# A language-model tower on one core: the gate and a test on GpSimd, the sum of the values from a column of ones, and another loop order

## The chip, the cores and the metric

The kernel runs on one NeuronCore of a Trainium2 chip. The metric is the device time of one execution in microseconds (us), lower is better. The engines are named as in the profile: PE (TensorE, matmuls; PEld is its weight loads), DVE (VectorE), ACT (ScalarE), POOL (GpSimd) and SP (SyncE, which here only issues DMAs).

## The reference, cut to what matters

```python
h = tok_ref(x, ...)                                  # two Mamba layers, 16 sequences of 128 tokens
h = h + attn_ref(_layernorm(h), w_qkv, w_proj, b_proj)
h = h + ffn_ref(_layernorm(h), w_in, g_in, w_out, g_out)

# one Mamba layer, D 192, D_INNER 384, D_STATE 16
xr, res = split(rmsnorm(x) @ in_proj_w)
xr = silu(causal_conv(xr, 4 taps) + conv_b)
dt, Bm, Cm = split(xr @ x_proj_w)
delta = softplus(dt @ dt_proj_w + dt_proj_b)
h_t = exp(delta * A) * h_{t-1} + delta * Bm * xr     # along the tokens, for each of 16 states
y = einsum(h, Cm) + xr * D
x = x + (y * silu(res)) @ out_proj_w                 # y * silu(res) is the gate below

# attention, 12 heads of 16, on each sequence
attn = relu(1 + qk + qk**2 / 2)                      # = ((1 + qk)**2 + 1) / 2
attn = attn / sum(attn);  out = (attn @ v) @ w_proj + b_proj

# feed-forward, 8-bit rounding of the rows, ternary weights
up, gate = split(quantised(rmsnorm(x, g_in)) @ w_in_q)
y = silu(gate) * up;  out = quantised(rmsnorm(y, g_out)) @ w_out_q
```

All matmuls of the layers and of the attention are float32; those of the feed-forward part are bfloat16 on small integers.

## The kernel before

The instructions of each engine are written out by hand in the order in which they run; semaphores join the engines, and there is no scheduler. The program has two stages.

**The chunk stage** (to about 256 us) does the two Mamba layers. A chunk is four sequences, 512 columns; there are eight: j = 0 to 3 are layer 0, j = 4 to 7 are layer 1. Inner channels are on the partitions in three groups c = 0, 1, 2. A loop `for i in range(...)` on each engine works on several chunks at once, each step with its own offset from i. Its steps for a chunk j:

- PE: `turn_in` (transposes of the scaled rows), `project_in(j, c)` and `project_gate(j, c)` (input projection, 96 + 96 rows), `project_x`, `project_steps`, `spread_b`, `spread_g`, `spread_c` (rows of B, B times C and C on all partitions), `count_below`, `project_out(j, 0/1)`.
- ACT: `first_tap`, `silu_input`, `take_xp`, `magnitude`, `positive_part`, `exponential`, `one_plus`, `logarithm` (these make delta), `decays`, `silu_gate_in`, `take_xt`, `square_sums`.
- DVE: `convolve` (three taps of each group), `error`, `delta`, `input_times_b`, `memoryless_states`, `scan_first`, `times_c`, `skip`, `b_times_c`, `scale`, `add_h`, and before the change also `gate` and `weakest_below`.
- POOL: `rest`, `step_times_input`, `add_first`, two small steps for the root of the mean square.

States 2 to 16 decay so fast that their old part underflows; `weakest_below`, `count_below` and `raise_flag` test that and set a flag, and `states_*` then skips the loop over them. With these inputs the loop is never run. PSUM has eight banks; each step's bank is a constant (`X_BANKS`, `Z_BANKS`, `S_BANKS`, ...), and a step waits until the bank's last user is done.

**The sequence stage** does attention and feed-forward, sequence by sequence (s = 0 to 15), with one prefix for each group g of four: `turn_x`, `project_qk`, `project_v`. For a sequence: `scores`, `square_scores`, `values`, `take_sums`, `turn_sums`, `divide`, `turn_attention`, `take_attention`, `project`, `add_attention`, `input_stats`, `input_gain`, `largest_input`, POOL's `input_root`, `input_most`, `input_step`, then `round_input`, `turn_input`, `take_input`, `project_up`, `silu_gate`, `hidden`, `gain`, `hidden_root`, `hidden_most`, `round_hidden`, `turn_hidden`, `take_hidden`, `project_down`, `add_ffn`, and the DMA of the result. The 1 in the square's expansion makes each score row need the plain sum of the values as well: `sum_tokens` (DVE) sums the rows over the tokens, `sum_values` (PE) multiplies them with the weights, `take_csum` keeps the sum, and `take_sums` (ACT) adds it as a bias while it empties the bank.

`keep_clock(n, b)` issues n matmuls of the identity with itself into bank b whose result nobody reads. They stand in the order after some of the waits, from the end of the chunk stage on.

## Time and profile before

| | |
|---|---|
| median of 3 runs | 413.48 us (413.07 to 415.75) |
| the profiled execution | 413.99 us, span 412.2 us, mean granted TensorE clock 0.967 |
| PE busy | 369.3 us, 90% of the span |
| PEld busy | 201.4 us, 49% |
| DVE busy | 320.7 us, 78% |
| ACT busy | 304.9 us, 74% |
| POOL busy | 200.1 us, 49% |
| DMA | 7.91 MB, nearly all before 50 us |

The span is from the first to the last instruction; 1.8 us of the profiled execution lie around it. A busy share is an average over two stages that have different limits. In a timeline a start and a duration are given; the duration of a DVE instruction reaches about 0.08 us into the next one, so what an instruction costs its engine is the distance of the starts. Float32 matmuls stand as two instructions each in the trace.

### The profile page before, as it was taken

The numbers are of one execution on the slowest core, as the hardware profiler recorded it, in microseconds if no ns is written. First come the engines' busy times: TensorE is split into PE (matmuls) and PEld (weight loads), VectorE is DVE, ScalarE is ACT, GpSimd is POOL, SyncE is SP. The second block draws the span as 40 slices with busy tenths as digits, with TensorE's granted clock in tenths as the row PEclk, the third lists the DMA queues.
The fourth block names the chain that finished last, engine by engine and source line by source line (L and its number), as shares of the span: only waits on it lengthen the run. The fifth ranks groups of instructions, "written<-read, shape, count | busy, mean of one in ns | idle before, by whom it ended". The sixth has DMA issues, their size and how long they took to land. (4 is left out here: it accounts for less than half of the span.)

```text
span 412.2 us, 6636 instructions
## 1 busy us (share of the span) xinstructions
PE 369.3 (90%) x1882; PEld 201.4 (49%) x1882; DVE 320.7 (78%) x687; ACT 304.9 (74%) x574; POOL 200.1 (49%) x300
## 2 busy tenths in 40 slices
PE   0398998999999999999998898999999999999774
PEld 0233333345354453453634537865765665566553
DVE  3069898799999999989999898454678667577752
ACT  2257999899999989899979792347686777478541
POOL 5537345535435345353653445012447564558872
PEclk9999696899999999999999999699899999999999
DMA  6743000000000000000000000000000000000001
GB/s 149 196 149 72 6 0 2 1 1 2 0 1 2 0 1 0 2 1 0 2 2 0 2 1 2 2 2 0 2 2 13 19 11 2 12 21 21 21 17 33
DMA packets 6879, 7.91 MB, mean 19 GB/s; under 512 B 1566, under 2 KB 5623, under 8 KB 6840
## 3 DMA queue, kind: packets, MB, share of 16 engines
q1 hardware_dynamic: 5238, 5.71, 5.0%
q0 software_dynamic: 768, 1.57, 1.8%
q8 instruction: 17, 0.28, 0.3%
q10 hardware_dynamic: 834, 0.17, 0.2%
q14 instruction: 22, 0.18, 0.1%
HBM read 5.87 MB, written 1.57 MB: 18 GB/s over the span
## 5 line engine op out<-in xcount | busy, mean ns | idle before, releaser
L751 PE MATMUL bank<-ring,win 96*128 96x512 f32 x192 | 99.8, 660 | 2.5 <-issue 1.2
L1468 POOL TENSOR_TENSOR du<-dl,pair 128x512 f32<-128x512 f32 x24 | 30.5, 1273 | 72.2 <-DVE dmin L1793 72.2
L751 PEld LDWEIGHTS bank<-ring,win 96*128 96x128 f32 x192 | 37.0, 207 | 57.6 <-issue 50.5
L1786 DVE SCALAR_TENSOR_TENSOR pair<-bank,cw,pair 128x508 f32<-128x508 f32 (+2 forms) x72 | 52.3, 736 | 10.5 <-ACT pair L311 8.6
L1473 POOL TENSOR_TENSOR arena<-arena 128x512 f32<-128x512 f32 x24 | 30.5, 1272 | 29.2 <-DVE arena L1827 29.2
L877 PEld LDWEIGHTS bank<-wout,pair 128*128 128x128 f32 x192 | 32.6, 199 | 10.5 <-issue 9.8
L1462 POOL TENSOR_TENSOR arena<-arena,dl 128x512 f32<-128x512 f32 x24 | 30.5, 1270 | 14.2 <-DVE dl L1778 14.2
L877 PE MATMUL bank<-wout,pair 128*128 128x192 f32 x192 | 37.1, 347 | 0.0
L499 ACT ACTIVATE du<-bank 128x512 f32<-128x512 f32 x48 | 25.1, 597 | 15.0 <-PE bank L983 7.6
L805 PE MATMUL bank<-dbl,wdt 13*128 13x512 f32 x48 | 27.4, 655 | 4.3 <-issue 1.3
L1814 DVE TENSOR_TENSOR_SCAN arena<-arena 128x512 f32<-128x512 f32 x24 | 29.2, 1217 | 0.0
L311 ACT ACTIVATE pair<-bank,cb,cw 128x512 f32<-128x512 f32 x24 | 18.6, 774 | 12.6 <-PE bank L751 12.6
L1528 POOL TENSOR_TENSOR pair<-pair,gout 128x512 f32<-128x512 f32 x16 | 20.5, 1284 | 7.7 <-issue 5.2
L788 PE MATMUL bank<-pair,wx 128*80 128x512 f32 x48 | 22.2, 599 | 2.0 <-ACT pair L345 1.8
L741 PE MATMUL bank<-ident,ring 128*96 128x128 f32 x64 | 9.2, 291 | 16.5 <-DVE ring L1764 16.5
L925 PE MATMUL bank<-ident 128*128 128x128 f32 x88 | 14.8, 295 | 8.9 <-ACT arena L555 3.1
L1793 DVE CUSTOM_DVE_ANT_0 dl<-du,arena 128x512 f32<-128x512 f32 x24 | 20.3, 845 | 1.4 <-issue 0.7
L341 ACT ACT_TABLE_LOAD x16 | 20.5, 1283 | 0.3
L1444 POOL DMA_INDIRECT h<-emb,idx x16 | 17.7, 1108 | 6.1 <-issue 4.3
L510 ACT ACTIVATE arena<-bank,csum 128x128 f32<-128x128 f32 x48 | 14.1, 368 | 7.7 <-PE bank L995 7.5
L925 PEld LDWEIGHTS bank<-ident 128*128 128x128 f32 x88 | 11.4, 190 | 14.7 <-ACT arena L555 4.5
L1778 DVE SCALAR_TENSOR_TENSOR dl<-du,dl 128x512 f32<-128x512 f32 x24 | 16.6, 692 | 2.0 <-ACT du L336 1.9
(183 smaller groups left out, 872.7 us busy)
## 6 DMA issues: line engine op xcount, KB each, us to landing
out<-h SPq DMA_DIRECT2D x16, 96.0 KB, 1.6
win<-in_w SPq DMA_DIRECT2D x2, 576.0 KB
arena<-ffn_in_t SPq DMA_DIRECT2D x1, 768.0 KB
wout<-out_w SPq DMA_DIRECT2D x2, 288.0 KB
arena<-ffn_out_t SPq DMA_DIRECT2D x1, 384.0 KB
wa<-w_qkv SPq DMA_DIRECT2D x1, 288.0 KB
wb<-w_qkv SPq DMA_DIRECT2D x2, 144.0 KB
h<-emb,idx POOLq DMA_INDIRECT x16, 6.5
```

What stands on the lines that cost most here:

```text
L341: nc.scalar.activation(du[:, j % NG, c, :], du[:, j % NG, c, :], ACT.Ln).then_inc(ln_done, 1)
L499: nc.scalar.activation(sq[s % 2][:, r, :], bank[:, SC_BANKS[r], :], ACT.Square, scale=HD ** -0.5, bias=1.0).then_inc(sq_ready, 1)
L751: last = nc.tensor.matmul(bank[:, b, :], win[:, j // NG, k, m * P:(m + 1) * P], xtr[:, j % 2, k, :], start=(k == 0), stop=(k == KH - 1))
L788: last = nc.tensor.matmul(bank[0:XM, XP_BANK, :], wx[:, j // NG, c, :], xc[:, j % NG, c, :], start=(c == 0), stop=(c == CI - 1))
L805: nc.tensor.matmul(bank[:, S_BANKS[c], :], wdt[DT_AT:DT_AT + R + 1, j // NG, c * P:(c + 1) * P], dbl[DT_AT:DT_AT + R + 1, j % 2, :], start ...
L877: last = nc.tensor.matmul(bank[:, T_BANK + b, i * D:(i + 1) * D], xc[:, j % NG, c, t0:t0 + LEN], wout[:, j // NG, c, :], start=(c == 0), s ...
L925: nc.tensor.matmul(bank[:, b, 0:P], ident[:, :], ident[:, :], start=True, stop=True)
L1462: nc.gpsimd.tensor_tensor(relu_s[:, c, :], relu_s[:, c, :], dl[:, j % NG, c, :], ALU.subtract).then_inc(rest_done, 1)
L1468: nc.gpsimd.tensor_tensor(du[:, g, c, :], dl[:, g, c, :], xc[:, g, c, :], ALU.mult).then_inc(du_ready, 1)
L1473: nc.gpsimd.tensor_tensor(yv[:, c, :], yv[:, c, :], bx[:, c, :], ALU.add).then_inc(yv_done, 1)
L1786: nc.vector.scalar_tensor_tensor(acc, seqs(bank[:, X_BANKS[c], :])[:, :, 0:LEN - tap], cw[:, j // NG, c, TAPS - 1 - tap:TAPS - tap], acc, ...
L1814: nc.vector.tensor_tensor_scan(bx[:, c, :], da[:, c, :], bx[:, c, :], 0.0, ALU.mult, ALU.add).then_inc(scan_done, 1)
```

## The change

Seven things are changed at once.

1. `gate` (a 128x512 multiplication for each chunk and group, 24 in all) and `weakest_below` (24 small ones) are moved from DVE to POOL.
2. The loop bodies of the chunk stage are in another order on every engine, with other PSUM banks and other waits that follow from them.
3. The sum of the values comes from `values` itself: the buffer of squared scores has a 129th column of ones, the matmuls have 129 columns, and `take_sums`, now on DVE, adds the last column to the others. `sum_tokens`, `sum_values`, `take_csum` and `spread_values` are gone.
4. In the sequence stage the 192 rows of a contraction are split 128 + 64 (`project_up` had 96 + 96). The two 64-row parts lie in different halves of the partitions and are issued one after the other. `take_x` copies twice instead of three times. The input projection of the chunk stage remains 96 + 96.
5. The `w_in` of the feed-forward part is laid out as 128 x 1536 instead of 96 x 2048 while it is made ternary.
6. `silu_gate` waits for both halves of `project_up`.
7. `keep_clock` is gone, and the order of the sequence stage is another one on every engine.

```diff
-X_BANKS = (3, 7, 4)
-Z_BANKS = (5, 7, 2)
-S_BANKS = (5, 6, 5)
+X_BANKS = (6, 2, 5)
+Z_BANKS = (3, 6, 3)
+S_BANKS = (5, 3, 7)
...
-                nc.scalar.activation(sq[s % 2][:, r, :], bank[:, SC_BANKS[r], :], ACT.Square, scale=HD ** -0.5,
-                                     bias=1.0).then_inc(sq_ready, 1)
-
-            def take_sums(s):
...
-                act.wait_ge(csum_out, s // SG + 1)
...
-                    nc.scalar.activation(nm[:, s % 2, c, :], bank[:, PV_BANK, c * P:(c + 1) * P], ACT.Identity,
-                                         bias=csum[:, s // SG % 2, c, s % SG:s % SG + 1]).then_inc(nm_out, 1)
+                    nc.scalar.activation(sq[s % 2][:, r, :, 0:P], bank[:, SC_BANKS[r], :].rearrange("p (j n) -> p j n", j=JH),
+                                         ACT.Square, scale=HD ** -0.5, bias=1.0).then_inc(sq_ready, 1)
...
             def project_in(j, c):
                 if c == 0:
-                    if j >= 2:
-                        pe.wait_ge(t_ready, 3 * (j - 1))
+                    if j >= 1:
+                        pe.wait_ge(dbl_ready, j)
+                        pe.wait_ge(bc_ready, j)
...
-            def keep_clock(n, b):
-                for _ in range(n):
-                    nc.tensor.matmul(bank[:, b, 0:P], ident[:, :], ident[:, :], start=True, stop=True)
...
-            def sum_values(g):
...
-                        last = nc.tensor.matmul(bank[j * HS:(j + 1) * HS, PV_BANK, c * P:(c + 1) * P],
-                                                va[b][:, i, c * JH + j, :], sq[s % 2][:, c, j * P:(j + 1) * P],
+                        last = nc.tensor.matmul(bank[j * HS:(j + 1) * HS, PV_BANK, c * (P + 1):(c + 1) * (P + 1)],
+                                                va[b][:, i, c * JH + j, :], sq[s % 2][:, c, j, :],
                                                 start=True, stop=True)
...
             def project_up(s):
                 pe.wait_ge(qxt_ready, s + 1)
-                for half in (1, 0):
-                    for k in range(KH):
-                        last = nc.tensor.matmul(bank[:, U_BANKS[half], :], qxt[:, s % 2, k, :],
-                                                wq1[:, k, half * F:(half + 1) * F], start=(k == 0), stop=(k == KH - 1))
-                    last.then_inc(up_ready, 1)
+                for k, half in enumerate((1, 0)):
+                    nc.tensor.matmul(bank[:, U_BANKS[half], :], qxt[:, s % 2, k, :], wq1[:, k, :], start=True, stop=False)
+                for k, half in enumerate((1, 0)):
+                    r = slice(64 * (1 - k), 64 * (2 - k))
+                    nc.tensor.matmul(bank[:, U_BANKS[half], :], qxt[r, s % 2, 1 - k, :], wq1[r, 2, :],
+                                     start=False, stop=True).then_inc(up_ready, 1)
...
+            def weakest_below(j):
+                if j >= 2:
+                    pool.wait_ge(count_ready, j - 1)
+                for c in range(CI):
+                    pool.wait_ge(delta_ready, 3 * j + c + 1)
+                    nc.gpsimd.tensor_scalar(below[:, j % 2, c:c + 1], dmin[:, j % 2, c:c + 1],
+                                            weakest[:, j // NG, c:c + 1], UNDERFLOW, ALU.mult,
+                                            ALU.is_le).then_inc(below_ready, 1)
+
+            def gate(j, c):
+                pool.wait_ge(scan_dve, (j + 1) * DECAYING * DVE_U)
+                pool.wait_ge(yv_done, 3 * j + c + 1)
+                pool.wait_ge(sz_ready, 3 * j + c + 1)
+                nc.gpsimd.tensor_tensor(xc[:, j % NG, c, :], sz[:, j % NG, c, :], yv[:, c, :],
+                                        ALU.mult).then_inc(gated, 1)
...
+            def ones_scores():
...
+                for b in range(2):
+                    nc.gpsimd.memset(sq[b][:, :, :, P:P + 1], 1.0).then_inc(ones_sq, 1)
...
+            def take_sums(s):
+                if s == 0:
+                    dve.wait_ge(wx_ready, 3)
+                if s >= 2:
+                    dve.wait_ge(nm_turned, s - 1)
+                dve.wait_ge(pv_ready, CH * s + CH)
+                for c in range(CH):
+                    at = c * (P + 1)
+                    nc.vector.tensor_scalar(nm[:, s % 2, c, :], bank[:, PV_BANK, at:at + P],
+                                            bank[:, PV_BANK, at + P:at + P + 1], None, ALU.add).then_inc(nm_out, 1)
```

**POOL in the loop of the chunk stage, before.** L1468 is `step_times_input`, L1462 `rest`, L1473 `add_first`, L1452 and L1457 the root of the mean square.

```order
L1468 TENSOR_TENSOR du<-dl,pair 128x512 x2
L1452 TENSOR_SCALAR ms<-ms 128x4
L1457 TENSOR_TENSOR rstd<-ms,neg_half 128x4
L1462 TENSOR_TENSOR arena<-arena,dl 128x512
L1468 TENSOR_TENSOR du<-dl,pair 128x512
L1473 TENSOR_TENSOR arena<-arena 128x512 x3
```

The same stretch after the change: L1347 is `gate`, L1339 `weakest_below`, L1332 `step_times_input`, L1326 `rest`, L1353 `add_first`.

```order
L1347 TENSOR_TENSOR pair<-pair,arena 128x512 x2
L1332 TENSOR_TENSOR du<-dl,pair 128x512
L1316 TENSOR_SCALAR ms<-ms 128x4
L1332 TENSOR_TENSOR du<-dl,pair 128x512
L1326 TENSOR_TENSOR arena<-arena,dl 128x512
L1321 TENSOR_TENSOR rstd<-ms,neg_half 128x4
L1332 TENSOR_TENSOR du<-dl,pair 128x512
L1347 TENSOR_TENSOR pair<-pair,arena 128x512
L1339 TENSOR_SCALAR below<-dmin,weakest 128x1 x3
L1353 TENSOR_TENSOR arena<-arena 128x512 x2
L1326 TENSOR_TENSOR arena<-arena,dl 128x512
L1353 TENSOR_TENSOR arena<-arena 128x512
```

Twelve full-size instructions a chunk stand there instead of nine, and the gates of groups 0 and 1 come before the next chunk's `step_times_input`, that of group 2 after it.

**PE where the chunk stage ends, before.** L829 is `spread_c(7)`, L941 and L946 `project_qk(0, t)`, L877 x12 `project_out(6, 0)` and `(6, 1)`, L955 and L960 `project_v(0)`, L925 `keep_clock`, L858 `count_below(7)`, L983 `scores(0)`.

```order
L941 MATMUL bank<-dl,wa 96x512 x2
L946 MATMUL bank<-dl,wb 96x512 x2
L829 MATMUL bank<-dbl,picked 128x512
L877 MATMUL bank<-wout,pair 128x192 x12
L955 MATMUL bank<-wa,dl 128x192 x2
L960 MATMUL bank<-wb,dl 128x192 x2
L955 MATMUL bank<-wa,dl 128x192 x2
L960 MATMUL bank<-wb,dl 128x192 x2
L925 MATMUL bank<-ident 128x128 x4
L858 MATMUL bank<-below,ones 128x1 x3
L983 MATMUL bank<-pair 128x256 x6
```

After the change, from `project_gate(7, 0)` and `(7, 1)` on: L674 `project_gate`, L754 `spread_c(7)`, L784 `count_below(7)`, L805 `project_out(6, 0)`, L852 `turn_x(0)`, L805 `project_out(6, 1)`, L862 and L865 `project_qk(0, 0)`.

```order
L674 MATMUL bank<-ring,win 128x512 x4
L754 MATMUL bank<-dbl,picked 128x512
L674 MATMUL bank<-ring,win 128x512 x2
L784 MATMUL bank<-below,ones 128x1 x3
L805 MATMUL bank<-wout,pair 128x192 x6
L852 MATMUL bank<-ident,ring 128x128 x8
L805 MATMUL bank<-wout,pair 128x192 x6
L862 MATMUL bank<-dl,wa 96x512 x2
L865 MATMUL bank<-dl,wb 96x512 x2
```

Before, both parts of `project_qk(0)` and all of `project_v(0)` stand ahead of `count_below(7)`. Now everything of the sequence stage stands behind it, and all three gate projections of chunk 7 are still to be done in its last round.

**PE at the very end, before.** L1046 is `project_down`, L1039 `turn_hidden`.

```order
L1046 MATMUL bank<-wq,arena 128x192 x4
L925 MATMUL bank<-ident 128x128 x4
L1039 MATMUL bank<-ident,pair 128x128 x4
L925 MATMUL bank<-ident 128x128 x2
L1046 MATMUL bank<-wq,arena 128x192 x4
L925 MATMUL bank<-ident 128x128 x3
L1039 MATMUL bank<-ident,pair 128x128 x4
L925 MATMUL bank<-ident 128x128 x2
L1046 MATMUL bank<-wq,arena 128x192 x4
```

And after: L951 `turn_hidden`, L958 `project_down`.

```order
L951 MATMUL bank<-ident,pair 128x128 x4
L958 MATMUL bank<-wq,arena 128x192 x8
L951 MATMUL bank<-ident,pair 128x128 x4
L958 MATMUL bank<-wq,arena 128x192 x4
```

The identity matmuls between a wait and the work behind it are gone (44 in the program), and two `project_down` now stand between the last two `turn_hidden`.

## Rows read from the trace of the kernel before

**Rows 1.** The page's part 2: granted TensorE clock in 40 slices of the span.

```profile
PEclk9999696899999999999999999699899999999999
```

**Rows 2.** Windows: us, busy us of each engine (count), granted clock, DMA share, GB/s.

```profile
57.10:220.00 162.90, 157.08 (x462) 72.01 (x461) 154.07 (x272) 150.13 (x253) 75.74 (x67) 0.97 0.00 1
...
118.97:145.64 26.67, 25.90 (x81) 12.26 (x80) 25.82 (x45) 25.56 (x44) 12.53 (x11) 1.00 0.00 1
...
259.90:267.30 7.40, 7.40 (x52) 5.90 (x55) 2.44 (x8) 1.57 (x3) 0.00 (x0) 0.55 0.00 0
...
262.00:380.00 118.00, 114.37 (x1017) 75.12 (x1015) 75.97 (x230) 78.91 (x183) 56.78 (x135) 0.97 0.03 9
380.00:412.20 32.20, 21.67 (x147) 15.40 (x145) 17.42 (x47) 13.44 (x29) 20.69 (x46) 1.00 0.07 23
```

**Rows 3.** Timeline of PE in a chunk: start, us, instructions of two group projections.

```profile
151.91 3.68 PE L751 MATMUL bank<-ring,win 96*128 96x512 f32 x8
```

**Rows 4.** Timeline of DVE in the same stage, start and us.

```profile
128.12 1.32 DVE L1793 CUSTOM_DVE_ANT_0 dl<-du,arena 128x512 f32<-128x512 f32 x1
...
130.88 0.68 DVE L1875 TENSOR_TENSOR pair<-pair,arena 128x512 f32<-128x512 f32 x1
131.48 0.69 DVE L1778 SCALAR_TENSOR_TENSOR dl<-du,dl 128x512 f32<-128x512 f32 x1
132.08 0.69 DVE L1793 CUSTOM_DVE_ANT_0 dl<-du,arena 128x512 f32<-128x512 f32 x1
```

**Rows 5.** Timeline of POOL beside it.

```profile
127.63 1.27 POOL L1462 TENSOR_TENSOR arena<-arena,dl 128x512 f32<-128x512 f32 x1 [1.46 <-DVE dl L1778]
```

**Rows 6.** Groups by line and shape: busy us, mean ns, idle before.

```profile
L1814 DVE TENSOR_TENSOR_SCAN arena<-arena 128x512 f32<-128x512 f32 x24 | 29.2, 1217 | 0.0
...
L1827 DVE SCALAR_TENSOR_TENSOR arena<-pair,dskip,arena 128x512 f32<-128x512 f32 x24 | 17.7, 738 | 0.0
...
L341 ACT ACT_TABLE_LOAD x16 | 20.5, 1283 | 0.3
...
L510 ACT ACTIVATE arena<-bank,csum 128x128 f32<-128x128 f32 x48 | 14.1, 368 | 7.7 <-PE bank L995 7.5
...
L1755 DVE TENSOR_SCALAR wq<-arena 96x2048 bf16<-96x2048 f32 x1 | 1.4, 1371 | 0.0
```

**Rows 7.** Timeline of PE at the start.

```profile
37.48 1.99 PE L751 MATMUL bank<-ring,win 96*128 96x512 f32 x4
...
41.48 6.97 PE L751 MATMUL bank<-ring,win 96*128 96x512 f32 x8
...
57.10 2.78 PE L788 MATMUL bank<-pair,wx 128*80 128x512 f32 x6
```

**Rows 8.** Timeline of PE where the chunk stage ends.

```profile
219.98 2.77 PE L788 MATMUL bank<-pair,wx 128*80 128x512 f32 x6
...
246.64 4.17 PE L877 MATMUL bank<-wout,pair 128*128 128x192 f32 x24
...
254.96 0.83 PE L858 MATMUL bank<-below,ones 128*128 128x1 f32 x6 [0.51 <-DVE below L1799]
...
268.33 0.52 PE L1003 MATMUL bank<-ident,arena 128*128 128x128 f32 x3
```

**Rows 9.** Timeline of DVE there: the last three gates.

```profile
257.68 1.89 DVE L1875 TENSOR_TENSOR pair<-pair,arena 128x512 f32<-128x512 f32 x3 [1.13 <-POOL arena L1473]
```

**Rows 10.** Timeline of PE in the sequence stage.

```profile
310.98 1.10 PE L946 MATMUL bank<-dl,wb 64*96 64x512 f32 x4
...
312.62 1.85 PE L971 MATMUL bank<-xsum,wvp 128*128 128x4 f32 x12
314.40 1.04 PE L1032 MATMUL bank<-wq,arena 96*128 96x512 bf16 x4
```

**Rows 11.** The chain that ended last, in order of time, near its end.

```profile
390.30 0.71 PE bank L925 x4
...
408.44 0.71 PE bank L925 x4
```

More of the change, by code:

```diff
@@ L1077, in _ @@
             project_qk(0, 1)
[L1078 to L1080 removed]
+            project_out(7, 0)
+            pe.wait_ge(sz_ready, 24)
+            pe.wait_ge(abs_done, 22)
+            pe.wait_ge(relu_done, 22)
+            pe.wait_ge(p_done, 24)
+            scores(0)
             pe.wait_ge(q_out, 4)
@@ L1154, in _ @@
             turn_attention(3)
+            pe.wait_ge(qxt_ready, 1)
+            turn_input(1)
+            pe.wait_ge(nm_out, 15)
+            values(5)
+            pe.wait_ge(att_out, 4)
+            turn_sums(4)
             pe.wait_ge(v_out, 4)
@@ L1956, in _ @@
-                if i - 4 in CHUNKS:
-                    add_h(i - 4, 0)
-                if i - 2 in CHUNKS:
-                    error(i - 2, 0)
+                if i - 2 in CHUNKS:
+                    delta(i - 2, 2)
+                    skip(i - 2, 1)
+                    scan_first(i - 2, 0)
+                if i - 1 in CHUNKS:
+                    b_times_c(i - 1)
+                if i - 2 in CHUNKS:
+                    times_c(i - 2, 0)
+                    scan_first(i - 2, 1)
+                    memoryless_states(i - 2, 2)
+                    times_c(i - 2, 1)
@@ L2109, in add_ffn @@
                                                ALU.mult, ALU.add).then_inc(h_out, 1)
+            convolve(6, 2, 1)
+            convolve(6, 2, 2)
+            input_times_b(5, 0)
+            convolve(6, 2, 3)
+            memoryless_states(5, 0)
+            input_times_b(5, 1)
+            memoryless_states(5, 1)
+            skip(5, 0)
+            scale(7)
+            delta(5, 2)
+            skip(5, 1)
+            scan_first(5, 0)
+            b_times_c(6)
+            times_c(5, 0)
+            scan_first(5, 1)
@@ L2129, in _ @@
-            gate(5, 1)
-            normalise(1)
+            memoryless_states(6, 1)
+            skip(6, 0)
+            delta(6, 2)
+            skip(6, 1)
             scan_first(6, 0)
-            gate(5, 2)
-            skip(6, 0)
-            normalise(2)
+            b_times_c(7)
+            times_c(6, 0)
             scan_first(6, 1)
-            delta(6, 2)
-            times_c(6, 0)
-            memoryless_states(6, 1)
+            memoryless_states(6, 2)
             times_c(6, 1)
+            error(7, 0)
@@ L2308, in _ @@
             round_input(7)
-            sum_tokens(3)
+            take_sums(10)
+            round_input(8)
             add_attention(9)
```

1398 lines of the change are left out of this document (624 added, 774 removed).

## The prediction

> **What bounds the kernel now.** I read the page's busy shares and its clock line first, then the windows by stage, then the timelines where the diff works. The clock line shows full speed but for a few dips [rows 1], so an answer per stage is possible, and there are three.
>
> In the chunk stage one undisturbed chunk takes 26.67 us, and PE is busy for 25.90 of them, DVE for 25.82, ACT for 25.56, POOL for 12.53 only [rows 2]. Three engines are full; relieving one of them leaves two. From `project_x(1)` at 57.10 to `project_x(7)` at 219.98 are 162.9 us, of which PE is busy 157.1 [rows 2, 7, 8]. In the sequence stage (262 to 380) PE has 114.4 of 118 us and the others 79 at most: PE alone bounds it. From 380 on PE has 21.7 of 32.2, nobody is full, and the end is a chain of short steps [rows 2], with `keep_clock` in it [rows 11].
>
> The sum below is made against the profiled execution, 413.99 us, which is 0.5 above the median of the runs.
>
> **Start.** The ternary preparation is four DVE passes over 2048 columns; one takes 1.37 [rows 6], so three quarters of the columns save about 4 x 1.37 x 1/4 = 1.4 us of DVE. But `project_in(1, 0)` now waits for `b_times_c(0)`, and that stands on DVE behind the preparation, near 41.0 by my walk, where it began at 37.48 before [rows 7]: PE stands idle some 3.5 us. The last eight input matmuls of chunk 1 took 6.97 us there at half clock, and 3.68 is what eight take at full clock [rows 3, 7]; with a pause ahead of them the half clock may come again. At full clock `project_x(1)` is reached at 56, at half clock near 62; I take 58.4: **+1.3 us**, with -1 and +5 as ends.
>
> **Chunk loop.** PE's work is the same, 157.1 us for the six chunks, a floor at -5.8. ACT loses two of its five table loads a chunk, 1.28 each [rows 6], so it comes to 23.0. DVE loses three gates, 0.60 from start to start each [rows 4], and the three small tests, 0.4: 2.2 together. What POOL gets is 3 x 1.27 (as its other full-size instructions, rows 5) + 0.6 = 4.4: 12.53 + 4.4 = 16.9 us.
>
> What speaks against this move is in the timelines. A `delta` usually starts 0.60 after its neighbour and is shown with 0.69, but one that started at 128.12, while POOL's `rest` ran from 127.63 to 128.90, is shown with 1.32 and ends 0.54 after POOL's [rows 4, 5]. I found ten such meetings in the stage, about one a chunk, each costing DVE 0.25 to 0.64, and no DVE instruction with two inputs from SBUF that ran through a POOL instruction at its usual speed. So each pair of engines' instructions of that kind must fit in one period: POOL 16.9, and DVE three times error 0.60, delta 0.60, scan 1.13 and skip 0.65 [rows 4, 6] = 8.9, and the scaling of a chunk's rows, under 1: 26.7 us at most. That is just over PE's 25.9. Not all has to be packed to the full, since a DVE instruction that reads PSUM may run beside POOL: DVE without its present stall and gates is 25.82 - 0.6 - 2.2 = 23.0; in the new order I count about four meetings of half a POOL instruction (0.64) = 2.5, so 25.5, still under PE. If three in five of the 12 instructions meet, it is 23.0 + 7.5 x 0.64 = 27.8. I take a period of 26.2, between PE's 25.9 and the port's 26.7; with 1.7 of PE's busy time over 6 x 25.9 it is 158.9 against 162.9: **-4.0 us**, ends -5.8 and +5.6.
>
> The Trainium skill, "SBUF — State Buffer", section "SBUF: two separate sides", describes this: DVE and GpSimd share one port pair under an exclusive lock, a DVE instruction with two SBUF inputs takes it only against a GpSimd instruction that reads SBUF, and the loser blocks for the whole instruction. The trace agrees (end 0.54 after POOL's end). By it alone and with no slack the period would be the port sum.
>
> **Transition**, from `project_x(7)` to the first `turn_sums`, 48.35 us before [rows 8]. `count_below(7)` ran at +35.0 and now comes at about +34.4, since the deltas of chunk 7 set it either way and PE is idle around it. Behind it stand now: `project_out(6, 0)` and `(6, 1)` at 2.1 each (two take 4.17, rows 8), `turn_x` 1.0, `project_qk` twice at 1.84 + 1.03 (a full part and a packed pair, rows 3, 10), 10.9 in all and 11.2 with a gap: `project_out(7, 0)` at +45.6. The gates are no longer DVE's three in 1.89 [rows 9], which ended at +39.6, but POOL's at 1.27 each, behind `add_first`, `ones_columns`, the root and `ones_scores`: they end near +43.1, late but hidden. Then `project_out(7, 0)` 2.1, `scores(0)` 1.1, `project_v(0)` 2.9, `project_out(7, 1)` 2.1, `values(0)` and part of `scores(1)` 1.6: +55.4. The half-clock stretch 259.9 to 267.3 (clock 0.55, rows 2) cost 7.4 x 0.45 = 3.3 and may come or not; I leave 1.0 for it. That is 56.4, or +8.0; one us comes back later, because `project_out(7, 1)` is then done: **+7.0 us**, ends +3 (no pause, full clock) and +10 (the half clock again).
>
> **Sequence stage.** PE-bound, so PE's work counts. `sum_values` goes: 1.85 each for the three groups of the stage [rows 10], -5.6. `project_up` has two full matmuls and a packed pair in place of four that take 1.04 [rows 10]; a packed pair of 64 rows takes 1.03 where four unpacked ones take 1.84 [rows 3, 10], so 0.1 to 0.2 a sequence, -2.7 for 16. That makes -8.3; the column of ones adds 12 columns' worth a sequence, next to nothing. ACT loses 48 `take_sums` of 0.37 [rows 6], DVE gets them for about as much less `sum_tokens`: 76 + 8 of 118 us, not the bound. I take **-7.5**; ends -3, if waits replace half of it, and -10, if the dip of the clock near 295 [rows 1] goes too.
>
> **Tail.** Ten `keep_clock` pieces stand on the chain from 390.3 to 409, 0.71 for most, 7.9 us in all [rows 11]. Without them PE has little to do there, and may fall to half clock: the rest of its work on the chain is 6 us, so up to +6, of which I take 4.5. `silu_gate` waits for the second half of `project_up` as well, +0.4 in all, and 1.0 because POOL's steps are next: -7.9 + 4.5 + 0.4 + 1.0 = **-2.0 us**, ends -7 and +1.
>
> **Sum:** 1.3 - 4.0 + 7.0 - 7.5 - 2.0 = -5.2, so 408.8 for the profiled execution and **408.3 us** for the median.
>
> **The rivals.** *The port binds the chunk loop.* For it: three engines at 96% and a POOL that collides whenever it is busy; against it: DVE's PSUM readers fit beside POOL. At a period of 27.8 the loop is 9.6 above my value: 417.9 us, slower than before; from 27.1 on (5.2 / 6 above 26.2) it decides the sign.
>
> *The half clock without `keep_clock`.* A stretch of 7 us at half clock costs 3.3 to 3.7 [rows 2, 3 and 7]. Two more of them than I took, at the start, the transition or in the tail, give 415.5 us. For it: the order before has identity matmuls just behind such waits; against it: the dips stood there in spite of them [rows 1].
>
> *Everything packs.* PE works through at full clock, 25.9 a chunk (-1.8 more), a transition at +4 (-3), the dip gone (-2), a tail at -5 (-3): 398.5 us. For it: the new order waits for fewer banks, and ACT and DVE both have 2.5 us of slack a chunk.
>
> *The sequence stage isn't bound by PE alone.* If DVE's share or the banks of `project_up` set the rate, the stage gives 2 instead of 7.5: 413.8 us, no change.
>
> **How the numbers follow.** Forecast 0.35, everything packs 0.25, the port 0.15, the half clock 0.12, the sequence stage 0.13. My forecast's own range is 404 to 412. About 1%, 409.3 to 417.6, is what a measurement of this kernel can tell from no change. Faster: all of packs and seven tenths of the forecast, 0.50; slower: a bit over half the port's and a part of the half clock's cases, which go above 417.6 only with the forecast's own errors, and something for what I haven't seen, 0.21; the rest 0.29. The range reaches from 398 to 418, which leaves out the upper half of the port's cases and the lower third of those in which everything packs.
>
> **What the profile after would show.** `project_x(1)` at 58.4 with an idle gap ahead of `project_in(1, 0)`; `project_x(7)` 158.9 later, one chunk at 26.2, POOL at 16.9 of them; DVE's delta, scan and skip with means above today's 1.22 and 0.74 where POOL runs beside them; the first `turn_sums` 56 after `project_x(7)`; a sequence at half a us less; a clock of 0.5 to 0.7 in the last 20 us. The prediction is wrong if the chunk period is not between 25.9 and 26.7, if PE still fills the transition, or if the tail keeps its clock.

## The result: 9% slower, with long stretches of PE at half clock

The changed kernel takes 450.18 us (449.41 to 451.36, 3 runs) against 413.48 before: a ratio of 1.0875, with an interval of 1.0803 to 1.0946. I had forecast 408.3, in a range that ended at 418. The profiled execution has a span of 447.6 us and a mean granted clock of 0.864 (412.2 and 0.967 before), and 379.0 us of PE busy time where 369.3 stood, although PE has less work.

The clock line of the page, to be laid beside [rows 1]:

```profile
PEclk9998589699955955999889667799999999999965
```

The windows by stage: us, busy us of PE, PEld, DVE, ACT, POOL (count of instructions), granted clock, DMA share, GB/s. The first goes from `project_x(0)` to `project_x(1)`, the next four are single chunks (2, 3, 4 and 5 of the eight), then comes the transition, then the stage of the sequences up to the last `turn_sums`, and the tail.

```profile
32.28:65.48 33.20, 29.16 (x53) 10.58 (x53) 21.33 (x36) 19.95 (x37) 14.40 (x13) 0.69 0.11 22
...
92.94:117.94 25.00, 24.25 (x81) 12.09 (x80) 22.92 (x37) 22.21 (x41) 21.37 (x17) 1.00 0.00 1
117.94:152.69 34.75, 34.17 (x81) 17.99 (x81) 25.55 (x40) 22.34 (x41) 21.27 (x17) 0.71 0.00 0
152.69:187.16 34.47, 34.11 (x81) 17.98 (x80) 25.06 (x39) 22.32 (x41) 21.27 (x17) 0.70 0.00 1
187.16:213.39 26.23, 24.56 (x81) 12.01 (x80) 25.22 (x39) 22.21 (x41) 21.28 (x17) 1.00 0.00 1
...
242.66:304.52 61.86, 48.80 (x202) 31.03 (x203) 41.46 (x82) 25.01 (x40) 36.01 (x32) 0.81 0.00 1
...
304.52:411.68 107.16, 100.20 (x920) 59.91 (x920) 79.82 (x250) 63.83 (x133) 54.67 (x131) 1.00 0.03 9
411.68:447.60 35.92, 20.02 (x97) 10.12 (x97) 18.40 (x50) 13.81 (x28) 20.52 (x47) 0.73 0.07 22
```

At full clock a chunk is shorter than before, 25.00 and 26.23 us against 26.67 [rows 2], and PE is busy for 24.25 and 24.56 us of it, not for 25.90. The largest part of that comes from the new order: it puts `project_steps(j, 2)` (13 rows) right ahead of `spread_g` (16 rows), and the two start within 0.01 us of each other. Before, the first two lines here, they stood 10 us apart, with 1.05 us of PE for each.

```profile
121.55 1.12 PE L805 MATMUL bank<-dbl,wdt 13*128 13x512 f32 x2
131.82 1.12 PE L823 MATMUL bank<-bc,not_first 16*128 16x512 f32 x2
...
102.93 0.69 PE L732 MATMUL bank<-dbl,wdt 13*128 13x512 f32 x1
102.94 0.69 PE L746 MATMUL bank<-bc,not_first 16*128 16x512 f32 x1
```

In chunk 3 the same 81 matmul instructions fill 34.17 us, at a clock of 0.71. Against before the difference is made up so (starts of the same work in both traces; the whole is 447.6 - 412.2 = 35.4):

| part | before | after | difference | forecast |
|---|---|---|---|---|
| to `project_x(1)` | 57.1 | 65.5 | +8.4 | +1.3 |
| `project_x(1)` to `project_x(7)` | 162.9 | 177.2 | +14.3 | -4.0 |
| to the first `turn_sums` | 48.35 | 61.9 | +13.5 | +7.0 |
| to the last `turn_sums` | 113.4 | 107.2 | -6.2 | -7.5 |
| to the end | 30.5 | 35.9 | +5.4 | -2.0 |

What stands ahead of a fall of the clock is plain in PE's timeline, here at the start of chunk 3's round: transposes, two `project_steps` of 13 rows, 0.58 us of waiting for `b_times_c`, and then `project_in`, which takes 3.45 us where 1.98 is usual.

```profile
120.54 1.04 PE L664 MATMUL bank<-ident,ring 128*96 128x128 f32 x8
121.51 1.98 PE L732 MATMUL bank<-dbl,wdt 13*128 13x512 f32 x4
124.06 3.45 PE L674 MATMUL bank<-ring,win 96*128 96x512 f32 x4 [0.58 <-DVE bc L1672]
```

Why was `b_times_c` late? On DVE it stands behind the first scan. In the chunk before, the scan took 1.23 us; here it takes 2.29, and `b_times_c` comes 5.3 us after `project_x` instead of 4.1:

```profile
95.80 1.23 DVE L1709 TENSOR_TENSOR_SCAN arena<-arena 128x512 f32<-128x512 f32 x1 [1.07 <-ACT arena L355]
97.06 0.68 DVE L1672 TENSOR_TENSOR bc<-dbl,bank 16x512 f32<-16x512 f32 x1
...
120.96 2.29 DVE L1709 TENSOR_TENSOR_SCAN arena<-arena 128x512 f32<-128x512 f32 x1
123.28 0.68 DVE L1672 TENSOR_TENSOR bc<-dbl,bank 16x512 f32<-16x512 f32 x1
```

On POOL `step_times_input` and the gate of group 2 run at that time:

```profile
120.45 1.72 POOL L1332 TENSOR_TENSOR du<-dl,pair 128x512 f32<-128x512 f32 x1 [2.54 <-DVE dmin L1695]
122.13 2.19 POOL L1347 TENSOR_TENSOR pair<-pair,arena 128x512 f32<-128x512 f32 x1
```

The scan is shown until 123.25, but by these rows the two engines take turns: the first POOL instruction ends 1.2 us after the scan's start, which is about what the scan is longer than its usual 1.22, and the gate is shown 0.9 longer than the 1.27 of POOL's full-size instructions before. That PE must wait for `b_times_c` at all comes from the new banks: bank 6 holds the result of `project_x` and then the first input projection of the next chunk (before: banks 4 and 3).

By group (busy us, mean ns, idle before), both sides pay now. POOL's instructions were 1270 long and the scan 1217 [rows 5, 6]:

```profile
L1332 POOL TENSOR_TENSOR du<-dl,pair 128x512 f32<-128x512 f32 x24 | 37.1, 1546 | 61.3 <-DVE dmin L1695 61.3
...
L1709 DVE TENSOR_TENSOR_SCAN arena<-arena 128x512 f32<-128x512 f32 x24 | 38.1, 1589 | 3.9 <-ACT arena L355 3.0
```

### The profile page after: what moved, and what is told of

Its sections match the earlier page's. It is cut to its first block and busy times, and to the rows that moved or that the text cites. A ratio compares the mean times of both kernels' runs of the same rounds, so it can differ in the third digit from the quotient of the medians.

```text
span 447.6 us, 6336 instructions
## 1 busy us (share of the span) xinstructions
PE 379.0 (85%) x1746; PEld 201.4 (45%) x1746; DVE 319.8 (71%) x672; ACT 266.9 (60%) x504; POOL 267.9 (60%) x350
## 5 line engine op out<-in xcount | busy, mean ns | idle before, releaser
L674 PE MATMUL bank<-ring,win 96*128 96x512 f32 x192 | 111.3, 725 | 9.5 <-issue 4.0
L1686 DVE SCALAR_TENSOR_TENSOR pair<-bank,cw,pair 128x508 f32<-128x508 f32 (+2 forms) x72 | 52.3, 738 | 31.1 <-ACT pair L299 25.8
L1332 POOL TENSOR_TENSOR du<-dl,pair 128x512 f32<-128x512 f32 x24 | 37.1, 1546 | 61.3 <-DVE dmin L1695 61.3
L674 PEld LDWEIGHTS bank<-ring,win 96*128 96x128 f32 x192 | 41.0, 227 | 72.3 <-issue 62.3
L805 PE MATMUL bank<-wout,pair 128*128 128x192 f32 x192 | 50.0, 429 | 0.0
L805 PEld LDWEIGHTS bank<-wout,pair 128*128 128x128 f32 x192 | 44.6, 259 | 7.8 <-POOL pair L1347 4.5
L1353 POOL TENSOR_TENSOR arena<-arena 128x512 f32<-128x512 f32 x24 | 36.4, 1530 | 9.2 <-DVE arena L1722 8.2
L1709 DVE TENSOR_TENSOR_SCAN arena<-arena 128x512 f32<-128x512 f32 x24 | 38.1, 1589 | 3.9 <-ACT arena L355 3.0
L1326 POOL TENSOR_TENSOR arena<-arena,dl 128x512 f32<-128x512 f32 x24 | 37.1, 1549 | 4.2 <-DVE dl L1678 4.2
L1347 POOL TENSOR_TENSOR pair<-pair,arena 128x512 f32<-128x512 f32 x24 | 36.6, 1537 | 4.9 <-DVEq L1735 4.9
L307 ACT ACTIVATE dl<-bank 128x512 f32<-128x512 f32 x24 | 14.1, 588 | 34.3 <-PE bank L732 34.3
L732 PE MATMUL bank<-dbl,wdt 13*128 13x512 f32 x48 | 28.6, 704 | 1.9 <-DVE arena L1703 1.2
L1775 DVE TENSOR_TENSOR h<-h,bank 128x384 f32<-128x384 f32 x16 | 8.8, 549 | 17.3 <-PE bank L805 16.3
L1394 POOL TENSOR_SCALAR ms<-mv 128x1 f32<-128x1 f32 x16 | 3.6, 227 | 28.8 <-DVE mv L1928 27.8
L509 ACT ACTIVATE pair<-bank,deq 128x512 f32<-128x512 f32 x16 | 11.0, 690 | 14.6 <-PE bank L945 7.2
```

The costliest lines, as they stand in the source:

```text
L674: last = nc.tensor.matmul(bank[:, b, :], win[:, j // NG, k, m * P:(m + 1) * P], xtr[:, j % 2, k, :], start=(k == 0), stop=(k == KH - 1))
L732: nc.tensor.matmul(bank[:, S_BANKS[c], :], wdt[DT_AT:DT_AT + R + 1, j // NG, c * P:(c + 1) * P], dbl[DT_AT:DT_AT + R + 1, j % 2, :], start ...
L805: last = nc.tensor.matmul(bank[:, T_BANK + b, i * D:(i + 1) * D], xc[:, j % NG, c, t0:t0 + LEN], wout[:, j // NG, c, :], start=(c == 0), s ...
L1326: nc.gpsimd.tensor_tensor(relu_s[:, c, :], relu_s[:, c, :], dl[:, j % NG, c, :], ALU.subtract).then_inc(rest_done, 1)
L1332: nc.gpsimd.tensor_tensor(du[:, g, c, :], dl[:, g, c, :], xc[:, g, c, :], ALU.mult).then_inc(du_ready, 1)
L1347: nc.gpsimd.tensor_tensor(xc[:, j % NG, c, :], sz[:, j % NG, c, :], yv[:, c, :], ALU.mult).then_inc(gated, 1)
```

## The experiments

Each ran with the kernel before on the same chip. "Loop" is the way from `project_x(1)` to `project_x(7)`, "transition" from there to the first `turn_sums`. Identity matmuls write to a place that nobody reads. Theory A is the clock: short waits of PE behind matmuls of few rows let it fall to half, and the loss is the time spent there. Theory B is the port: DVE and POOL hold each other up, and that by itself is the loss.

**e1, b_times_c early.**

```diff
-                    scan_first(i - 2, 0)
                 if i - 1 in CHUNKS:
                     b_times_c(i - 1)
+                if i - 2 in CHUNKS:
+                    scan_first(i - 2, 0)
```

> The changed kernel with one move: on DVE b_times_c of the next chunk stands ahead of the first scan of this one, not behind it. Theory A (the clock): in the changed kernel bank 6 holds both the result of project_x and the first input projection of the next chunk, so PE waits for b_times_c right behind two matmuls of 13 rows; where a scan that POOL holds up (2.29 us instead of 1.22) delays b_times_c, PE stands idle for 0.4 to 0.6 us and then runs at half clock for 7 to 21 us (from 76, 124, 158.7 and 219.5). Without that wait these stretches should be gone: the way from project_x(1) to project_x(7), 177.2 us, falls to 155 to 162, and the whole from 450.2 to about 432. Theory B (the port): the loop is long because DVE and POOL hold each other up, wherever b_times_c stands; the move changes less than 3 us.

Measured: 436.62 us, a ratio of 1.0489 (1.0421 to 1.0556). The loop fell from 177.2 to 163.7 us, most of it in chunk 3:

```profile
119.67:145.78 26.11, 24.54 (x81) 12.15 (x81) 24.44 (x39) 22.23 (x41) 21.07 (x17) 1.00 0.00 0
```

34.75 became 26.11 by one instruction's place. POOL's means did not change (1545); the scan's fell from 1589 to 1416, some 0.5 us of DVE a chunk, so most of what the move gained was the clock. Beside the stretch of chunk 1, two shorter ones stayed (from 160 and from 208), the first behind a wait of 0.85 us for another instruction of DVE, the second behind steps with no wait at all. The loop is just above what A had forecast (155 to 162): the wait is a trigger and not the only one.

**e2, gates back on DVE.**

```diff
+                if i - 2 in CHUNKS:
+                    gate(i - 2, 0)      # on DVE, (i - 2, 1) and (i - 2, 2) a little behind
```

> The changed kernel with the 24 gates back on DVE, behind the flag's test of their chunk; everything else as changed. Theory A: the scan ahead of b_times_c is not held up any more, PE doesn't wait there, the clock stays: project_x(1) to project_x(7) about 160, the whole about 430 to 435. Theory B: POOL's full-size instructions go back from a mean of 1.54 to 1.27 us and the scans from 1.59 to 1.22, and the loop gains that alone, 1.5 to 3 us a chunk, at full clock too: a chunk at full clock (25.0 now) becomes shorter than 25. By A a chunk at full clock becomes longer, 25.5 to 26.5, because DVE gets 1.8 us.

Measured: 442.57 us, 1.068 (1.0616 to 1.0745), one run at 436.8 and one at 445.2. The loop is 170.5, with chunks of 26.15 to 31; no chunk fell to 34. Nearly full clock gave 26.15, longer than 25.0, as A says. But POOL's means stayed at 1.55 and 1.76, and the scan's at 1.51: the gates aren't the only ones that meet. B's numbers failed. A's premise failed too: PE still waited four times for `b_times_c`, 1.7 us in all, the clock fell five times more after the stretch in chunk 1, and the loop is 10 us longer than forecast. So this run does not decide between the two.

**e3, the tests back on DVE** (`weakest_below` behind `delta(j, 2)`).

> The changed kernel with weakest_below (72 instructions of one column) back on DVE, right behind the last delta of its chunk; the gates stay on POOL. Where the chunk stage ends PE stands idle for 6.98 us until POOL has done step_times_input, a gate and the three tests. Theory A: the transition (61.9 us from project_x(7) to the first turn_sums) falls by 4 to 5 us for the wait and by 3 more if the half-clock stretch behind it goes; the loop is as it is; the whole 440 to 446. Rival: the deltas of chunk 7 are what is late, and the test on DVE only waits in another queue: less than 2 us.

Measured: 451.51 us, 1.0852 (1.0791 to 1.0912), the transition 61.7. PE's wait for the test fell from 6.98 to 0.80 us, but 1.97 for a gate and 4.84 for the normalisation of the first rows stood behind it. The rival's number is right and its reason is not: `count_below(7)` came 6.8 us earlier (+28.98 against +35.75), so the deltas were not what was late. The next waits took the gain.

**e4, the kernel before without `keep_clock`.**

> The kernel before without its 44 identity matmuls, nothing else. If they are what keeps the clock up, the last 31 us fall to a clock near 0.7 as in the changed kernel and the transition gets a longer stretch at half clock: 414 to 425. If they only cost PE's time on the chain (7.9 us in the tail), it is 406 to 411.

Measured: 417.88 us, 1.0046 (1.0015 to 1.0077). Its last 31.8 us run at 0.64, its transition takes 51.8 us (48.35). In the tail identities and half clock cost the same; 3.4 us are lost in the transition.

**e5, b_times_c(0) early too.**

```diff
                 if i == 1:
+                    b_times_c(0)
                     weight_magnitudes()
                     ternary_weights()
```

> The kernel of e1 (b_times_c ahead of the first scan) in which b_times_c(0) stands ahead of the ternary preparation too (PE waits for the sum of the weights before it writes bank 7 again). In the changed kernel PE is idle for 4.03 us ahead of project_in(1, 0) and then at half clock to 59.5. If that wait is what costs the start its 8.4 us, project_x(1) comes at 57 to 60 instead of 65.5, and the time falls 6 to 8 us below e1's. If the half clock there comes from PE's idle time before (28 to 32 us, waiting for the first silu), the gain is the wait alone, 3 to 4 us.

Measured: 436.03 us, 1.0525 (1.045 to 1.06); `project_x(1)` at 66.9. A miss of my own making: PE waits for the sums of `weight_magnitudes` ahead of the steps, and these were now later.

**e6, identities behind the steps.**

```diff
                     project_steps(i - 2, 1)
+                    for _ in range(6):
+                        nc.tensor.matmul(bank[96:128, XP_BANK, 0:P], ident[:, 96:128], ident[:, :], ...)
                 if i - 1 in CHUNKS:
                     project_in(i - 1, 0)
```

> The changed kernel with six matmuls of 32 columns of the identity (128 rows, nobody reads them) behind project_steps(j, 1), ahead of the wait for b_times_c. Nothing is undone of the gates, the order or the waits. Theory A (the clock): if short idle time behind matmuls of few rows is what lets the clock fall, these fill it, and the loop loses the two stretches of 20 us at half clock: 155 to 163 for the loop instead of 177.2, the whole about 435. Theory B (a wait that costs by itself): nothing changes, or 0.5 us a chunk is added.

Measured: 430.84 us, 1.0397 (1.0299 to 1.0495), 19 us less than the changed kernel with more work for PE. The clock line, and one of four like chunks:

```profile
PEclk9997569689999999999998795999999999999955
```

```profile
119.85:146.07 26.22, 25.68 (x93) 13.42 (x92) 25.02 (x39) 22.21 (x41) 21.20 (x17) 1.00 0.00 1
```

From 89 to 230 us the clock never falls; the loop is 159.5 us. Waits, gates and banks were as changed, and DVE and POOL still held each other up as much (the scan's mean is 1622, POOL's 1546), so B is out as the cause of the long loop.

**e7, identities in the tail** (26 of them, in pairs and threes as before).

> The changed kernel with 26 identity matmuls in its last 35 us, two or three ahead of a matmul that has just been waited for, as before. In the changed kernel the clock is 0.70 from 415 on and the way from the last turn_sums to the end takes 35.9 us (30.5 before). If the half clock costs more there than the identities, it falls by 3 to 5 us and the clock is 1.00; if not, it stays within 1 us.

Measured: 450.29 us, the same as the changed kernel. The last 31.8 us, at full clock:

```profile
416.70:448.50 31.80, 19.10 (x129) 12.65 (x128) 14.57 (x37) 11.93 (x25) 17.45 (x38) 1.00 0.07 23
```

The tail is not long by its clock.

**e8, covers everywhere.** The edits of e5 and e7, more identities, and the tests and `add_h(5)` at other places.

> All together on the changed kernel: b_times_c early (e5), four identity matmuls of 32 columns behind project_steps(j, 1) and behind spread_g, the three tests on POOL ahead of step_times_input(j, 2) and the gate, add_h(5) behind delta(7, 1), 12 identity matmuls ahead of count_below(7), and those of e7 in the tail. If the clock is what the change lost, the loop comes to 150 to 156 us (25 to 26 a chunk), project_x(1) to 58, the transition to 50 to 54, and the sum to 402 to 412: below the kernel before. If the order itself is worse, it stays above 418.

Measured: 440.46 us, with runs from 434.0 to 448.5, too far apart for an interval. In the profiled run the loop was 159.2, with chunks 3, 4 and 5 at 26.2, the transition 61.2, `project_x(1)` at 68.4. By its time it is the second answer, above 418; by its parts the loop was mended and the rest not.

**e9, gates on POOL in the kernel before.**

```diff
+                if i - 3 in CHUNKS:
+                    gate(i - 3, 0)      # on POOL; (i - 3, 1) and (i - 3, 2) between the step_times_input
                 if i - 2 in CHUNKS:
                     rest(i - 2, 1)
```

> The kernel before with 21 of its 24 gates (all but those of chunk 7) on POOL, between rest, step_times_input of the next chunk; nothing else is changed. The port theory alone: POOL's full-size instructions go from 1.27 to about 1.5 us and the scans from 1.22 to about 1.5, DVE gains nothing: a chunk is as long as before or longer (26.7 to 28), the whole 413 to 422. If DVE's relief of 1.8 us a chunk counts: 26 a chunk, about 409. PE's order and its banks are those of before here, so that the clock should fall no more often than before.

Measured: 421.76 us, 1.0184 (1.0126 to 1.0243). The window of a chunk, and the scans of the whole run:

```profile
142.77:170.05 27.28, 25.85 (x80) 12.25 (x81) 26.11 (x42) 25.27 (x44) 17.35 (x14) 1.00 0.00 0
```

```profile
L1834 DVE TENSOR_TENSOR_SCAN arena<-arena 128x512 f32<-128x512 f32 x24 | 32.7, 1363 | 1.2 <-ACT arena L367 1.2
```

27.28 at full clock against 26.67 [rows 2]: in the old order DVE does 1.8 us less a chunk and is busy for longer (26.11 to 25.82), since its instructions wait for POOL. So DVE's relief is used up and 0.6 us a chunk more, which is small beside the clock's price. The whole loss is larger, 8.1 us: 5.0 in the loop, where one chunk of 28.97 has a clock of 0.94, and 2.7 in the transition, at a clock of 0.90.

**e10 and e11, start and transition covered**, both on e6: 20 identities ahead of `project_x(0)` with the `b_times_c(0)` of e5, and 22 in the round of chunk 7.

> The kernel of e6 with b_times_c(0) ahead of the ternary preparation and 20 identity matmuls in the idle time ahead of project_x(0) (28 to 32 us). In e6 project_x(1) comes at 66.5, with half clock at 30 to 37 and 44 to 61. If PE's idle time lets the clock fall there, project_x(1) comes at 56 to 60. If it is the low rows of what PE does there (transposes, steps), it stays above 63 and the way from project_x(0) is 33 us or more.

> The kernel of e6 with identity matmuls in the last round of the chunk stage: 4 ahead of project_x(7), 6 behind it, 12 ahead of count_below(6). In e6 the transition is 59.8 us with half clock at 232 to 239, 242 to 245 and 256 to 267. If the clock makes it long, it falls to 51 to 55 (my forecast of 55.4 was at full clock); if the order does (turn_x behind the scans of chunk 7 and the normalisation), it stays at 58 to 60.

Measured: e10 433.92 us (427.0 to 437.0), `project_x(1)` at 67.4, behind the same wait for the sums as in e5, 3.13 us. e11 427.6 us, 1.0318 (1.0264 to 1.0373), the transition 57.5 at a clock of 0.91 (59.8 in e6), between the two answers: most of it stays.

**e12, combined.**

> All that should help, on the changed kernel: b_times_c early everywhere, 3 identity matmuls behind the steps, the start of e10, the last round of e11, the tests ahead of step_times_input on POOL and add_h(5) behind delta(7, 1). If the clock is the cause of the loss in every part: project_x(1) at 58, the loop 153 to 157, the transition 52 to 55, the rest 143, in all 408 to 414, level with the kernel before. If a part stays long for another reason: 418 to 430.

Measured: 429.88 us, 1.038 (1.0329 to 1.0431). The loop was 157.8, `project_x(1)` came at 67.1 as in e10, and the transition was 59.7: the second answer, 418 to 430.

**e13, the start mended.** As e10, but on DVE:

```diff
                     weight_magnitudes()
+                    b_times_c(0)
                     ternary_weights()
```

> The kernel of e10 in which b_times_c(0) stands on DVE behind weight_magnitudes and ahead of ternary_weights. In e10 b_times_c(0) stood ahead of weight_magnitudes, and PE waited 3.13 us for the sums of the weights behind it, a wait of my own making. Theory A: without any wait of PE between project_x(0) and project_in(1, 1) the clock stays and project_x(1) comes at 54 to 58 (66 to 67 in e6 and e10), and the whole 8 to 10 us below e6. Rival: the rows of PE's work at the start (13 and 16 of 128) let the clock fall even without a wait, and it stays above 62.

Measured: 423.08 us, 1.0253 (1.0215 to 1.029), `project_x(1)` at 54.8. The window from `project_x(0)` on, to be compared with 33.20 at 0.69 above:

```profile
31.85:54.80 22.95, 21.46 (x65) 9.02 (x65) 20.31 (x34) 19.81 (x38) 14.78 (x13) 1.00 0.16 32
```

Between e10 and e13 lies the place of one instruction, and `project_x(1)` comes 12.6 us earlier by it.

**e14, all mended.**

```diff
+                if i - 2 == NJ - 1:
+                    decays(i - 2, 0)    # ACT, ahead of the gates of chunk 7
+                    decays(i - 2, 1)
...
             normalise(0)
+            normalise(1)                # DVE, ahead of the scans of chunk 7
+            normalise(2)
+            normalise(3)
```

> The kernel of e12 with the start of e13, and in the transition decays(7, 0) and (7, 1) on ACT ahead of the gates of chunk 7 and normalise(1) to (3) on DVE ahead of the scans of chunk 7. In e11 and e12 DVE stands idle for 4 us until decays(7, 0) is done, which stands behind the three gates, and PE for 5 us until normalise(3), which stands behind the scans. If the order there is what makes the transition long, it falls from 57 to 60 to 49 to 53; with project_x(1) at 56 and a loop of 154 to 156 that is 403 to 408 in all, below the kernel before. If only one of them works, 410 to 418.

Measured: 419.31 us, 1.0158 (1.0134 to 1.0183), the transition 56.6 at a clock of 0.88. Both waits were gone, others of 1.4 to 2.1 us for POOL's test and gate took their place. It is above both ranges that I had given.

**e15, the kernel before covered.**

> The kernel before with six identity matmuls ahead of project_steps(0, 2) and eight ahead of project_steps(1, 1), where PE stands idle for 0.92 and 1.34 us just before it runs at half clock for 7 and 10 us (41.5 to 48.4 and 65 to 75). If idle time behind matmuls of few rows lets the clock fall there as well, both stretches go and the time falls by 6 to 9 us; if not, it is the same or up to 1 us longer.

Measured: 420.25 us, 1.0075 (1.0033 to 1.0118), with runs from 415.4 to 427.0. A clear miss: the clock fell again, once with PE busy without a gap:

```profile
36.18 1.98 PE L805 MATMUL bank<-dbl,wdt 13*128 13x512 f32 x4
38.09 2.73 PE L751 MATMUL bank<-ring,win 96*128 96x512 f32 x4
```

and the added wait for `xt_ready` made PE idle for 2.03 us in the round of chunk 1. Idle time just ahead is not needed for a fall: PE had worked without a gap from 32.48 us on, and the clock fell at 39.2.

**e16, the start alone** (e13's move on the changed kernel, no identities).

> The changed kernel with nothing but the start of e13: b_times_c(0) on DVE between weight_magnitudes and ternary_weights, no identity matmuls anywhere. If PE's wait of 4 us for b_times_c(0) alone costs the start, project_x(1) comes at 55 to 58 instead of 65.5 and the time falls by 8 to 10 us (the loop behind it may fall differently). If the identity matmuls ahead of project_x(0) were needed as well, it comes at 60 or later.

Measured: 439.1 us, but its four runs lie between 429.3 and 453.9, so that only the trace can be read, and as one run among them: `project_x(1)` at 62.4. PE has no gap behind `project_x(0)` there and the clock falls all the same, at 40. The move is worth 3 us alone in this one trace, and 12 with identity matmuls ahead of it (e6 to e13).

**e17, chunk 1 filled** (ten identities where later rounds have a `project_out`).

> The kernel of e13 with ten identity matmuls in the round of chunk 1 at the place where later rounds have a project_out (between count_below and project_steps(1, 2)). In e13 the clock falls at 68 for 10 us, in that round alone: there the steps of 13 rows follow each other with no project_out between, and PE waits 0.62 and 1.10 us. If the missing work lets the clock fall there, the stretch goes, the way from project_x(1) to (2) is 25 to 26 us instead of 28.6, and the time falls by 2.5 to 3.5 us. Otherwise it is the same.

Measured: 418.46 us, 1.011 (1.0077 to 1.0143). The way from `project_x(1)` to (2) went from 28.6 to 27.4; the stretch at half clock got shorter (74 to 78) and did not go, so the way gained 1.2 us where about 3 were expected. The medians lie further apart (423.08 and 418.46), but the profiled runs only 1.0.

**e18, all of it.**

> The kernel of e14 with six instead of three identity matmuls behind the steps, the ten of e17, and eight each ahead of project_gate(7, 2) and of count_below(7), where e14 ran at half clock from 239 to 253. If the clock is all that is left, the stretches at 60 to 79, 166 to 175 and 239 to 253 go: 419.3 less 3, 2.5 and 4 to 6, so 408 to 411, below the kernel before. If the transition stays long for its order, 412 to 416.

Measured: 413.11 us in 12 runs, against 413.72 of the kernel before beside it, 1.0021 (0.9985 to 1.0058): no difference.

```profile
PEclk9999989999999999999999979999999999999955
```

```profile
211.38:267.95 56.57, 49.91 (x272) 34.27 (x271) 40.59 (x82) 26.22 (x41) 36.27 (x30) 0.94 0.00 1
```

`project_x(1)` comes at 54.5 (57.1 before), the loop takes 156.9 (162.9), the transition 56.6 (48.35), the rest 143.2 (143.9). The 36 us of the changed kernel are given back by the places of some ten instructions and by identities for PE, and the gates are still on POOL. The transition did stay long, as the second range said (412 to 416).

## Why the prediction was wrong, by its own steps

**Start, +1.3 forecast, +8.4 measured.** The step saw the wait for `b_times_c(0)`: 4.03 us where I had 3.5, and `b_times_c` at 42.87 where I had 41.0.

```profile
43.65 3.75 PE L674 MATMUL bank<-ring,win 96*128 96x512 f32 x4 [4.03 <-issue]
```

I had written that at half clock `project_x(1)` comes near 62, and took 58.4. Both the choice between the ends and the upper end itself were wrong: the stretch at half clock lasted 17 us, from 42.5 to 59.5. In e13, with the wait gone and identity matmuls ahead of `project_x(0)` and behind the steps, the clock is 1.00 and the whole term is gone (54.8). How it divides between the wait and the half clock is open, since the move alone was seen in one trace only (e16, 3 us).

**Chunk loop, -4.0 forecast, +14.3 measured: the step that failed.** "PE's work is the same, 157.1 us" was wrong in both directions. At full clock PE needs 24.25 us for a chunk and not 25.9, so the floor was none: I had not seen that `project_steps(j, 2)` and `spread_g` would run side by side, which accounts for 1.05 of the 1.65 us. The period was 25.0 and 26.2 where I said 26.2 and had called anything outside 25.9 to 26.7 a sign of being wrong; the 25.0 is outside. The port's upper end of 27.8 did not come; in e12 and e18 most chunks take 25.7 to 25.8. What cost the time is that four stretches at half clock came in the loop, of 10, 21, 20 and 7 us (from 76, 124, 159 and 220). The first has its like before, from 65 to 75; the other three are new, and the loop's matmuls filled 170.3 us of PE instead of 157.1. I had looked for meetings of DVE and POOL only as time on DVE, and never asked who waits behind a scan that is held up: `b_times_c`, and by the new banks PE, right behind its matmuls of 13 rows. e1 shows 13 us of it and e6 18, which is the whole distance from -4.0 to +14.3. My rival of the half clock had the right mechanism in the wrong places, and "two more of them" was its size; it was 0.12 of the chances.

**Transition, +7.0 forecast, +13.5 measured.** The order's part was seen in the main: e18, at a clock of 0.94, still needs 8.2 us more than before. The half clock is a part of the rest, of which I left 1.0: e11 covered it with the order as it was and gained 4.3 of the 13.5. e18 also moved instructions, so that the exact share is not shown. `count_below(7)` came at +35.8 where I had +34.4, behind the longest wait of PE, for POOL's tests:

```profile
278.41 1.44 PE L784 MATMUL bank<-below,ones 128*128 128x1 f32 x6 [6.98 <-POOL below L1339]
```

Behind it stood 1.42 us of waiting ahead of the second `project_qk(0)`, which my sum left out. And a second chain was as late as this one: where the wait for the tests was shortened (e3, e12), `turn_x(0)` waited 4.84 and 4.42 us for `normalise(3)`, which stands behind the scans of chunk 7, the first of which waited in e12 for `decays(7, 0)` behind the three gates' `silu_gate_in`.

**Sequence stage, -7.5 forecast, -6.2 measured.** Near, with PE busy for 100.2 instead of 109.1 us, but with some luck in it: the dip of the clock near 295, which my -7.5 left out, is gone too. It lasted 3.5 us, so by my estimate it is worth up to 1.8, and the work itself gave about 4.4.

**Tail, -2.0 forecast, +5.4 measured.** I took `keep_clock` out of the chain and put half clock in. e7 shows that these two weigh the same: that is 3.4 of the 7.4 us missed. What I did not count is how much is left at the last `turn_sums`: eight `project_down` and not seven, all through bank 1 one after the other with what reads it, and two `project_down` between the last two `turn_hidden`. So the sequence stage's gain was given back: from the first `turn_sums` to the end it is 143.1 us for 143.9. That the order alone does this was read from the traces and not tried by itself.

**The port.** That DVE waits for POOL was read rightly from [rows 4, 5], and e9 gives its price in the old order: 0.6 us a chunk, with DVE's relief of 1.8 already counted against it. The Trainium skill ("SBUF — State Buffer", section "SBUF: two separate sides") says that the loser blocks for the whole instruction. The rows above agree in both directions: the scan takes 2.29 us behind a POOL instruction, and POOL's gate behind the scan 2.19 where POOL's full-size instructions took 1.27 before. As a sum over a chunk, 26.7 in the prediction, it did not bind: one chunk of the changed kernel took 25.0, four in e18 25.7 to 25.8. The sum had counted POOL's small instructions as well, and a scan that ran beside two of the three tests took its usual time:

```profile
98.37 1.22 DVE L1709 TENSOR_TENSOR_SCAN arena<-arena 128x512 f32<-128x512 f32 x1
98.19 1.50 POOL L1339 TENSOR_SCALAR below<-dmin,weakest 128x1 f32<-128x1 f32 x2
```

**What stays open.** How long a stretch at half clock lasts: 7, 10, 20 and 21 us, all with PE busy throughout once it had started again, and no row tells why the one ends and the other doesn't. And why the clock held at 192.7, where the same steps, the same long scan (2.29 us) and a wait of 0.61 us stand as at 124 and 158.6:

```profile
193.29 1.96 PE L674 MATMUL bank<-ring,win 96*128 96x512 f32 x4 [0.61 <-DVE bc L1672]
```

Nor is it shown which of the two lets the clock fall, the wait or the few rows ahead of it. e6's identities take away both at once, and no run fills the wait with matmuls of few rows.

## What to carry to other kernels

When a change moves work between engines, follow each instruction that gets slower to the one behind it in its queue, and from there to the engine that waits: here, in chunk 3, 1.07 us on a scan became 0.58 us of idle PE and 9 us of time. Where PE is the bound, its busy time isn't a constant: look at what it does ahead of each fall of the clock in the trace before, and count how many such places the new order makes. A shared PSUM bank is a wait, and which wait it is belongs into the sum. And the same matmuls in another order can take less of PE, where two of few rows come to stand side by side.

## What the runs showed of the hardware that I had not expected

In the chunk loop the clock fell with waits of only 0.36 to 0.58 us (at 124, 159 and 220 in the changed kernel), and also with none (at 39 in e15, at 62 in e14), each time within 3 us of matmuls of 13 or 16 rows. Such matmuls stand in every chunk, and behind most of them it held. Six identity matmuls of 128 rows and 32 columns there held it for 140 us (e6); three did so in e12, beside an earlier `b_times_c`, and failed twice in e14, at 62 and 167.

Two float32 matmuls of 13 and of 16 rows, issued one after the other, started within 0.01 us of each other and are shown with 1.13 us together (102.93 to 104.06), where each alone is shown with 1.12.

Kernels with such places don't repeat equally well: e16's runs are 25 us apart, while the changed kernel, one instruction's place away from it, repeats within 2.
